# GpSimd's two gather stages in a graph network kernel: its program in a loop with a ring of indices, or written out with the indices read from the table

## What is computed

```python
def _L0_gnn_ref(x, W1, b1, W2, b2, edge_index):
    dst, nbr = edge_index[0], edge_index[1]
    agg = jax.ops.segment_sum(x[nbr], dst, num_segments=n)          # gather of 53125 rows
    mean = agg / jnp.maximum(cnt, 1.0)[:, None]
    return x @ W1.T + b1 + mean @ W2.T + b2

def _L1_gnn_ref(x, W, a, src, dst):
    h = jnp.einsum('ni,hio->nho', x, W)
    hs, hd = h[src], h[dst]                                         # gather of 53125 rows
    ...                                                             # a score per edge and head
    att = e / (s[src] + EPS)                                        # softmax over each node's edges
    return jax.ops.segment_sum(att[..., None] * hd, src, num_segments=n)

x = x + _L0_gnn_ref(_layernorm(x), ..., edge_index)
x = x + _L0_ffn_ref(_layernorm(x)[None], ...)[0]                    # 8 experts, top 2
x = x + _L1_gnn_ref(_layernorm(x), ..., src, dst)
x = x + _L1_ffn_ref(_layernorm(x)[None], ...)[0]                    # 16 experts, top 2
```

## Time and profile before

| what | us |
|---|---|
| median of 3 runs | 3132.11 |
| lowest and highest of them | 3130.18, 3142.37 |
| the profiled execution: its span, from the first to the last instruction | 2743.5 |
| median less this span | 388.6 |

### The profile page before, as it was taken

The page is one execution under the profiler, slowest core; times in us unless marked ns, Lnnn a source line. Parts: engine busy times, 40 slices in busy tenths (PEclk is TensorE's granted clock), DMA queues, the critical chain, the costliest instruction groups (busy, mean ns, idle before and its releaser), DMA issues. The chain is left out here.

```text
span 2743.5 us, 60771 instructions
## 1 busy us (share of the span) xinstructions
PE 2153.7 (79%) x15045; PEld 1753.1 (64%) x15046; DVE 1635.8 (60%) x4124; ACT 1456.4 (53%) x3571; POOL 1398.2 (51%) x1441
## 2 busy tenths in 40 slices
PE   4789965676776589999935889888884989669990
PEld 3666633444444479999934878888873777559990
DVE  7889953333333643333356877878777878854337
ACT  6779943333333334343437766666665888433335
POOL 0000067777777223333314777777761999335540
PEclk9989987666666689999968999999985999879995
DMA  3310036533333511111133778888782888452224
GB/s 112 100 51 21 25 118 196 166 104 105 105 104 103 139 44 38 35 37 34 35 115 106 233 238 239 236 247 241 240 207 68 280 269 258 167 209 71 70 65 146
DMA packets 182508, 368.83 MB, mean 134 GB/s; under 512 B 30426, under 2 KB 67716, under 8 KB 182126
## 3 DMA queue, kind: packets, MB, share of 16 engines
q1 hardware_dynamic: 118489, 208.65, 22.4%
q0 software_dynamic: 53760, 148.67, 20.5%
q10 hardware_dynamic: 10133, 9.97, 1.1%
HBM read 275.35 MB, written 91.83 MB: 134 GB/s over the span
## 5 line engine op out<-in xcount | busy, mean ns | idle before, releaser
L939 PE MATMUL sum_ps<-weightsL_w 128*128 128x256 f32 x880 | 370.1, 571 | 179.0 <-DMA weightsL_w<-y_gnn,sum_index 97.6
L843 POOL DMA_INDIRECT scores_rows<-h_gnn,scores_index x440 | 425.3, 967 | 132.5 <-issue 126.4
L843 POOL DMA_INDIRECT weightsL_w<-y_gnn,sum_index x440 | 418.2, 950 | 138.2 <-issue 127.7
L939 PEld LDWEIGHTS sum_ps<-weightsL_w 128*128 128x128 f32 x880 | 225.1, 280 | 323.7 <-issue 291.1
L954 DVE TENSOR_TENSOR sums_acc<-sums_acc,sum_ps 128x256 f32 x440 | 185.3, 421 | 364.0 <-PE sum_ps L939 321.0
L1598 ACT ACTIVATE sums_acc<-expertsL_hid_ps,expertsL_b 128x128 f32<-128x128 f32 x704 | 197.7, 372 | 299.8 <-PE expertsL_hid_ps L1547 299.5
L1547 PE MATMUL expertsL_hid_ps<-sums_acc,expertsL_w 128*128 128x128 f32 x2816 | 337.1, 277 | 4.2 <-DVE sums_acc L1618 3.0
L2089 PE MATMUL scores_diff_ps<-all_ident,scores_rows 128*128 128x128 f32 x880 | 296.5, 337 | 51.3 <-DMA scores_rows<-h_gnn,scores_index 38.2
L1547 PEld LDWEIGHTS expertsL_hid_ps<-sums_acc,expertsL_w 128*128 128x128 f32 x2816 | 327.0, 193 | 4.7 <-issue 4.6
L1522 POOL DMA_INDIRECT ys_L<-sums_acc,ffnL_result x120 | 145.0, 1209 | 355.1 <-DVE sums_acc L1628 334.3
L1559 PE MATMUL expertsL_out_ps<-weightsL_w,sums_acc 128*128 x1408 | 323.6, 379 | 0.0
(11 more groups left out here) (438 smaller groups left out, 4183.9 us busy)
## 6 DMA issues: line engine op xcount, KB each, us to landing
saved_gnn<-scores_rows SPq DMA_DIRECT2D x220, 264.0 KB
sum_rows<-saved_gnn SPq DMA_DIRECT2D x220, 264.0 KB, 3.1
weightsL_w<-in_L_ffn_W SPq DMA_DIRECT2D x16, 1024.0 KB, 9.2
weightsL_w<-in_L_ffn_w SPq DMA_DIRECT2D x32, 512.0 KB, 8.8
scores_lanes<-slot_lanes SPq DMA_DIRECT2D x44, 320.0 KB, 5.1
sort_low_b<-low_lanes SPq DMA_DIRECT2D x32, 416.0 KB, 3.5
weightsL_w<-ys_L SPq DMA_DIRECT2D x6, 1280.0 KB, 11.8
weightsL_w<-y_gnn,sum_index POOLq DMA_INDIRECT x440, 2.8
```

Source lines behind the costliest of these rows:

```text
L843: pool.indirect_dma_start(out=self.rows[s] if isinstance(self.rows, list) else self.rows[:, s, :], out_offset=None, in_=table[:, :], in_of ...
L939: last = nc.tensor.matmul(ps[s % banks][:, 0:D], pick[h][:, s % HALF, :], g.rows[s], start=True, stop=True)
```

## The change

The ring `index`, its semaphore and the counter go. `pool` is a plain Python loop over 22 turns, so that GpSimd's program has 440 indirect DMAs one after the other in each stage. The waits for `freed` stand where they stood, with constants. Each indirect DMA takes its indices from column k = 20 x turn + slot of `slot_dst` itself. Everything else, the gathers' sources, targets, order and semaphores among it, is as before.

```diff
--- before.py
+++ after.py
@@ -816,38 +816,19 @@
     def __init__(self, m, width, parts=(HALF,), rows=None):
         self.parts = parts
         self.rows = m.sb("rows", [P, SLOTS, width]) if rows is None else rows
-        self.index = m.sb("index", [P, 2, SLOTS], I32)
-        self.index_ready = m.sem("index_ready")
         self.width = width
         self.landed = [m.gather_sem(f"landed{p}") for p in range(PAIRS)]
         self.freed = m.sem("freed")
-        self.tick = m.sem("gather_tick")
 
     def pool(self, nc, pool, e, table):
-        turns = Q // SLOTS
-
-        def bring(turn, b):
-
-            nc.gpsimd.tensor_copy(self.index[:, b, :], e["slot_dst"][:, bass.ds(SLOTS * turn, SLOTS)]).then_inc(self.index_ready, 1)
-
-        def gather(turn, b, last):
-            starts = [h * HALF + sum(self.parts[:n]) for h in range(2) for n in range(len(self.parts))]
+        starts = [h * HALF + sum(self.parts[:n]) for h in range(2) for n in range(len(self.parts))]
+        for turn in range(Q // SLOTS):
             for n, start in enumerate(starts):
                 pool.wait_ge(self.freed, len(starts) * turn + n + 1)
-                if n == 0:
-                    pool.wait_ge(self.index_ready, turn + 1)
-                pool.sem_inc(self.tick, 1)
                 for s in range(start, start + self.parts[n % len(self.parts)]):
-                    if s == SLOTS - 1 and not last:
-                        bring(turn + 1, 1 - b)
+                    k = SLOTS * turn + s
                     pool.indirect_dma_start(out=self.rows[s] if isinstance(self.rows, list) else self.rows[:, s, :], out_offset=None, in_=table[:, :],
-                                            in_offset=bass.IndirectOffsetOnAxis(ap=self.index[:, b, s:s + 1], axis=0)).then_inc(self.landed[s // 2], 16)
-        bring(0, 0)
-        with pool.Fori(0, turns // 2 - 1) as i:
-            for b in range(2):
-                gather(2 * i + b, b, False)
-        for turn in range(turns - 2, turns):
-            gather(turn, turn % 2, turn == turns - 1)
+                                            in_offset=bass.IndirectOffsetOnAxis(ap=e["slot_dst"][:, k:k + 1], axis=0)).then_inc(self.landed[s // 2], 16)
 
 
 def tiles_of(nc, engine, e, first, count):
```

## The result

The kernel after took 3073.34 us in the median of four runs (3067.57 to 3087.47), the kernel before, run beside it, 3131.14 us (3110.86 to 3142.37): a ratio of 0.985 with a 95% interval of 0.981 to 0.989. (A ratio is always a kernel's time by that of the kernel before on the same chip, with its 95% interval in brackets.) On two further chips the ratio was 0.993 (0.990 to 0.995) and 0.992 (0.989 to 0.994). Why the gain is twice as large on the first chip isn't shown.

A forecast was written before the change was run, and what follows sets the result against it. GpSimd's gather pace was taken to bound both gather stages; savings of 2.0 us (stage 1 copies), 2.1 us (stage 2 copies) and 0.4 us (stage 2's first gather), 4.5 us in all, gave 3127.6 us, range 3115 to 3141.

The forecast's parts named there:

- What bounds the kernel: Both gather stages: GpSimd starts a gather every 1.25 us without a break, 550 us of their 559 and 560.
- outside the span: 388.6 us between span and median time; 0 taken for program growth there, upper bound 4.6 us.
- The loop, its counter with it: GpSimd in both gather stages: branches, register waits and counter increments gone, gain 0; uncovered branches 3 us a stage.
- The copies: GpSimd, 22 index copies a stage at 0.10 us a turn: gain 2.0 us in stage 1, 2.1 in stage 2.
- no stall takes this back: Stage 2: the copies' 2.1 us stays gained, since turn 1's slots are freed 5.3 us before they are needed.
- Direct reading: Gathers of both stages take indices from the 448-wide table: cost 0, upper bound 32 ns more a gather.
- a median above 950 ns: Gathers of both stages: sign that the forecast is wrong; their median was expected still at 946 ns.
- rival 2: Both gather stages: each direct gather 32 ns dearer, 28.2 us less 4.5, giving 3155.8 us; chance 0.08.
- Program size: GpSimd's written-out gathers, 720 more instructions: 0 within the span; late program could cost 6.6 us a stage.
- None of the five: Rivals: nothing comes through 0.15; dearer direct gathers 0.08; copies' whole cost 0.05; gap goes 0.01; branches hold GpSimd up 0.03.
- Rival 5: GpSimd in both gather stages: each of 20 taken branches costs 0.30 us, 6 us, giving 3121.6 us; chance 0.03.

The follow-up runs named there:

- the one long profiled execution: Profiled run, 3167.55 us, of the kernel after with GpSimd's 132 counter increments behind its waits put back; that kernel took 3139.41 us, ratio 1.004.
- The edit of 88 increments alone: Kernel after with GpSimd's counter increment behind each wait put back in stage 2 only: 3143.60 us, ratio 1.004.
- the ring kernel: Kernel before with GpSimd's program written out, ring and copies kept, 132 counter increments left out: 3082.67 us, ratio 0.986; on another chip 3116.13 us, 0.996.

## Why the prediction was wrong

**What bounds the kernel: wrong, and the source of the rest.** The step was "both stages run at GpSimd's pace". It is true of the execution in the earlier trace rows and of no later profile. The sign was there: 388.6 us between span and median. The prediction named them, called them "outside the span", and priced only a growth of 4.6 us in them. In all later profiles the span and the execution's own time differ by 2 us, so those 388.6 us were time inside the stages that the shown execution didn't have. 111 of the 328 us by which the spans differ lie in stage 1 (670.4 against 559) and 216 in stage 2 (776.5 against 560).

**The loop, its counter with it: the term that failed.** "I take 0, hidden behind the gather in work." The prediction listed the increments of a counter among what goes and priced the lost cover by the branches alone, 10 at 0.30 us. The cover is gone at every real wait: ScalarE releases, GpSimd has nothing in work, and wait, increment and gather follow one another. Measured, 0.52 us in each of some 60 waits of stage 2, 31 us. Over all these traces stage 2 takes 808 to 854 us in the seven with increments on GpSimd (mean 824.7) and 771 to 794 us in the eleven without that leave the rest of stage 2 alone (mean 785.4), with no overlap; the difference is 39 us, of which the 31 are shown by the release rows and 8 are not placed. Without the one long profiled execution, 853.6 us, the first mean is 819.9 and 3 to 4 us are left. Part of the difference may come about by way of TensorE's clock: in stage 2 the granted clock is 0.74 to 0.76 in the mean in the seven traces and 0.77 to 0.80 in the eleven. The edit of 88 increments alone moved it from 0.77 to 0.75, so the clock followed the increments; what it added to them isn't separated. Stage 1 doesn't gain: 680 us in the mean of the five with increments there, 688 in the nine without that otherwise have its program of before or after. 39 us less in stage 2 and 7 more in stage 1 make 32 us, 1.0% of 3130, between the ratios found.

**The copies: price possible, effect not seen.** 0.10 us each was read from a stream without waits. With them and the loop's increments kept out (two runs of the ring kernel) the gain is there; with them gone and the increments kept, it isn't. In stage 2 GpSimd stands for over 230 us, so 0.10 us saved between two gathers can be waited away; "no stall takes this back" was read from the trace in which GpSimd waited 2.1 us for ScalarE in all:

```profile
  ACT scores_ends L2150: 2.1, 7
```

Forecast 4.5 us; what can be told apart here is larger than that.

**Direct reading: within its bounds, but past its own mark.** 7 and 11 ns a gather, inside the 0 to 32 of the prediction, nearer 0. 440 x 0.007 + 440 x 0.011 = 7.9 us of GpSimd's time, hidden for the same reason. But by the prediction's own figures this was a sign of being wrong: it named a median above 950 ns as one, and the medians are 953 and 957; and it let rival 2 decide from 5 ns a gather, where the price eats the whole gain of 4.5 us. That it didn't show in the time is due to the waits, which the prediction didn't have: rival 2 would have wanted a GpSimd that never waits.

**Program size: right.** 5 more packets of program than before on the second of the two instruction queues (q14, 70 against 65) and no pause in the gathers that isn't a wait for slots: outside the first gather of each part of slots, the longest gap between two is 0.44 us.

```profile
q8 instruction: 61, 1.00, 0.1%
q14 instruction: 70, 0.57, 0.1%
```

**Rivals.** None of the five named what happened. Rival 5 came nearest: something of the sequencer's, a fixed price at certain places. It looked at the branch, where the trace has nothing, and not at the wait. The kernel with the ring written out has no branches, and its ratio is 1.000 (0.997 to 1.003): nothing shows of a stall at each branch, though 6 us lie within that interval.

## What to carry to other kernels

Compare the profiled execution's span with the median time before reading anything else; if they differ by more than a few us, the waits of that trace aren't those of the timed kernel, and a forecast from it needs a range that says so. A wait that ends last should sit on the instruction that it guards: here one cheap instruction between the wait and the gather cost 0.52 us at each of 60 waits, and writing the loop out paid only together with letting that instruction go. (On ScalarE and TensorE some 970 such instructions cost 21 to 27 us in all, so the price is not the same everywhere.) Engines that release buffers should do it by the semaphore that their work already increments: taking out the wait for oneself and the second semaphore, with the release by pairs that came with it, brought the ratio to 0.970 and 0.975. On the chip where the ring kernel without increments ran beside it, that is 3039.04 against 3082.67 us, another 1.4%, as much as the change itself.

## What was unexpected

- The same kernel shows a span of 2743.5 us in one trace and 3141.4 us in another, with equal work. The difference is in waits on semaphores: VectorE's additions of stage 1 wait 321.0 us in 207 waits of at most 5.3 us in the first, and 301.3 us in 51 waits, up to 10.3 us, that the profile can put down to nobody, besides 194.4 us put down to "issue" and TensorE, in the second. The granted clock in stage 2 is 0.92 in the mean in the first and 0.75 in the second, which may be the effect of the waits as well as a cause. What the first execution lacked isn't known, and no run here brought it back.
- The stops of stage 1 stay when VectorE's register loads go or its program becomes a loop, and move within the turn when the slots are released otherwise. Late completions of TensorE's matmuls would fit, since the products were made up to 16 us before; no experiment took them away. Stage 2 has such stops too, on ScalarE, which also makes the releases that GpSimd waits for; they are longer in total than anything the change gained, and no run tested them. In the kernel after:

```profile
ACT scores_size L2138 <- remote: 313.2, 51, 16.6
```

- The Trainium skill ("NOTIFIC — the notification-queue block", 7.1 Overflow) describes a setting in which recording holds the engines up when its queue is full; whether that happens in these runs can't be told: there is a span and a clock on record for each of them, and no run without recording to hold against them.
- Increments between gathers that don't wait cost nothing that shows (808.1 us in stage 2 with one per gather, 817.1 to 853.6 with one per wait), a first one behind a wait 0.52 us, a second 0.08.
- The part between the two gather stages, untouched by every edit, takes either 580 to 587 us or 595 to 600 us from stage 1's last gather to stage 2's first, in kernels of both kinds. This alone moves a run by 0.3 to 0.6%, and wasn't followed up.
